# Accumulating DMAs for the sums of a two-gate attention and feed-forward layer, with vector work moved between batches

## The reference

```python
def _bi_wkv(r, k, v, w, u, time_emb):
    tf = sigmoid(sum(time_emb, -1))
    decay = exp(-exp(w)) * (0.5 + 0.5 * tf)
    ek = exp(min(k, 30)); ekv = ek * v
    # a[t] = a[t-1] * decay + ekv[t]; b the same with ek; once forward, once backward in time
    nf, df = scan(step, (ekv, ek)); nb, db = scan(step, (ekv, ek), reverse=True)
    euk = exp(min(u + k, 30))
    num = nf + nb - ekv + euk * v
    den = df + db - ek + euk
    return sigmoid(r) * (num / max(den, 1e-8)) * (0.8 + 0.2 * tf)

# attention: qkv = x @ w_qkv.T + b_qkv; causal softmax(q k / 4) v; @ w_out.T + b_out
# ffn: w -> clip(round(w / mean|w|), -1, 1) * mean|w|; (silu(x @ up) * (x @ gate)) @ down
```

## Time and profile before

| | |
|---|---|
| median of 3 runs | 182.76 us (182.74 to 183.18) |
| the profiled execution, its whole time | 182.91 us |
| its span (first to last instruction) | 181.1 us |
| outside the span | 1.8 us |
| DVE busy | 156.2 us, 86% of the span |
| PE busy | 147.6 us, 82% |
| ACT busy | 114.7 us, 63% |
| POOL busy | 51.1 us, 28% |

### The profile page before, as it was taken

One profiled execution on the slowest core, in us unless ns is written; L12 is line 12 of the kernel. 1 busy time (PEld: TensorE's weight loads), 2 busy tenths in 40 slices (PEclk: granted clock), 3 DMA queues, 4 the chain that ended last, 5 costly groups with the idle time before them and its releaser, 6 DMA issues. The chain is left out here.

```text
span 181.1 us, 3815 instructions
## 1 busy us (share of the span) xinstructions
PE 147.6 (82%) x1544; PEld 97.6 (54%) x1544; DVE 156.2 (86%) x262; ACT 114.7 (63%) x181; POOL 51.1 (28%) x49
## 2 busy tenths in 40 slices
PE   0008597973999889999899689997998999997991
PEld 0008483331348656764576357744764676785880
DVE  0699958999999979999998999999769999986672
ACT  2638756999777743589357634883593348885550
POOL 8700032999700049340000194400002223000000
PEclk9999789999699999999999999999999999999999
DMA  4999204000000400000132000000420000010001
GB/s 100 360 430 424 108 29 145 4 0 2 0 5 0 173 5 0 0 5 0 58 103 76 0 4 0 2 4 4 144 87 0 0 5 4 4 62 2 4 0 58
DMA packets 5706, 10.91 MB, mean 60 GB/s; under 512 B 760, under 2 KB 4024, under 8 KB 5304
## 3 DMA queue, kind: packets, MB, share of 16 engines
q1 hardware_dynamic: 5400, 10.52, 15.4%
q10 hardware_dynamic: 288, 0.14, 0.5%
HBM read 6.43 MB, written 1.05 MB: 41 GB/s over the span
## 5 line engine op out<-in xcount | busy, mean ns | idle before, releaser
L245 POOL TENSOR_TENSOR extra<-extra,k_t 128x512 f32<-128x512 f32 x7 | 8.9, 1268 | 84.3 <-DVE fwd L589 40.9
L676 DVE TENSOR_REDUCE row_max<-wide 128x4 f32<-128x1024 f32 (+1 forms) x24 | 28.8, 1216 | 0.6 <-PE wide L1039 0.6
L437 ACT ACTIVATE silu<-attn_ps,up_scale 128x256 f32<-128x256 f32 x24 | 11.2, 473 | 24.6 <-PE attn_ps L986 22.1
L399 ACT ACTIVATE probs<-wide 128x1024 f32<-128x1024 f32 x24 | 23.9, 1020 | 3.2 <-PE wide L1064 2.6
L589 DVE TENSOR_TENSOR_SCAN fwd<-decay,ek 128x256 f32<-128x256 f32 x32 | 21.1, 704 | 0.0
L601 DVE TENSOR_TENSOR_SCAN bwd<-ek,decay 128x255 f32<-128x255 f32 x32 | 21.1, 706 | 0.0
L270 POOL TENSOR_TENSOR hid_lo<-hid,hid_hi 128x512 f16<-128x512 f32 x9 | 12.4, 1380 | 14.3 <-ACT hid_hi L444 14.3
L1184 PE MATMUL wide<-ones 128*128 128x128 f32 x24 | 4.5, 369 | 14.1 <-DVE fwd L776 14.1
L986 PE MATMUL attn_ps<-x_lo,w_tern 128*128 128x256 f16 x96 | 13.9, 273 | 1.2 <-DVE x_lo L701 1.2
L986 PE MATMUL attn_ps<-x_hi,w_tern 128*128 128x256 f16 x96 | 14.3, 274 | 0.0
L1034 PE MATMUL wide<-mask_qk,identity_b 128*128 128x256 bf16 (+1 forms) x48 | 11.0, 311 | 3.6 <-DMA stack<-halves 1.9
(11 more groups left out here) (144 smaller groups left out, 343.3 us busy)
## 6 DMA issues: line engine op xcount, KB each, us to landing
stack<-halves SPq DMA_DIRECT2D x24, 128.0 KB, 2.1
w_raw<-wup_d SPq DMA_DIRECT2D x1, 1024.0 KB, 11.5
w_raw<-wgate_d SPq DMA_DIRECT2D x1, 1024.0 KB, 13.2
w_raw<-wdown_d SPq DMA_DIRECT2D x1, 1024.0 KB, 15.0
out_d<-x_t SPq DMA_DIRECT2D x4, 256.0 KB, 2.3
wqkv<-wqkv_d SPq DMA_DIRECT2D x1, 768.0 KB, 7.2
k_t<-k_d SPq DMA_DIRECT2D x1, 768.0 KB, 8.6
x_t<-x_d SPq DMA_DIRECT2D x1, 768.0 KB, 10.0
```

What stands on the lines that cost most here:

```text
L399: nc.scalar.activation(probs[:, j, :], flat(wide[j % 2][:, :, :]), ACT.Exp, scale=SOFTMAX_SCALE).then_inc(prob_done, 1)
L437: nc.scalar.activation(silu[:, e % 2], up, ACT.Silu, scale=up_scale[:, 0:1]).then_inc(silu_done, 1)
L676: nc.vector.tensor_reduce(out, src, AX.X, ALU.max).then_inc(max_done, 1)
```

## The change

Seven edits, in neutral terms:

1. Ten of the large adds become DMAs that GpSimd issues with `accum_op=ALU.add`: `send_extra` and `send_backward` for gate 0 of batches 2 and 3 (`by_dma`) and gate 1 of batches 0 to 2. A gate's second DMA waits for the first. `sums` of these gates and their `add_extra` leave the compute engines. Gate 1 of batch 3 keeps both adds on the vector engine.
2. The two products of batch 0 (`values_of_keys(0)`, `extra_products(0, 0)`) move from the vector engine to GpSimd, and half of the small decay and gain instructions stand behind `first_gate(0)`.
3. Scans move between turns: gate 0's of the next batch leave the block of `maxima` and `gate`, and stand at the border; in the last turn gate 1's backward scans stand around the border, and its forward scans inside the block.
4. `ffn_input` now writes f32 `x2`; ScalarE copies it to `x2_hi` (`high_input`); `low_input` subtracts.
5. ScalarE: `minus_maxima(0)` moves ahead of the second `ternary_weights`, the third goes to turn b = 1 ahead of the first silu, `key_exp(3)` moves two exponentials later. Its list has the second gate's reciprocal ahead of the row sums' in every turn, as before.
6. TensorE: three more filler products of `ones` behind the first twelve, released by `recn_done[0]`; in turn b = 1 the first `up_gate` products of `x2_hi` stand ahead of the scores.
7. The last network's last block is split in two pieces (`tail_halves`).

```diff
@@ when a DMA adds, and who waits for it
+        def by_dma(c, b):
+            return b >= 2 if c == 0 else b < B - 1
+        def wait_summed(engine, c, b):
+            if by_dma(c, b):
+                engine.wait_ge(sum_in[c], 16 * (b - 1 if c == 0 else b + 1))
+            else:
+                engine.wait_ge(sum_done[c], b + 1 if c == 0 else 1)
...
@@ gpsimd
-            def add_extra(c, b):
+            def send_extra(c, b):
                 pool.wait_ge(prod_done[c], b + 1)
                 pool.wait_ge(fwd_done[c], 4 * b + 4)
-                nc.gpsimd.tensor_tensor(fwd[c][:, :, :], fwd[c][:, :, :], extra[c][:, :, :],
-                                        ALU.add).then_inc(fwd_extra[c], 1)
+                pool.dma_start(fwd[c][:, :, :], extra[c][:, :, :], accum_op=ALU.add).then_inc(extra_in[c], 16)
+            def send_backward(c, b):
+                wait_extra_added(pool, c, b)
+                pool.wait_ge(bwd_done[c], 4 * b + 4)
+                pool.dma_start(fwd[c][:, :, :], bwd[c][:, :, :], accum_op=ALU.add).then_inc(sum_in[c], 16)
...
+            values_of_keys(0)
+            extra_products(0, 0)
             pool.wait_ge(blank, 3)
...
@@ scalar
+            def high_input(b):
+                for ct in range(CT):
+                    act.wait_ge(x2_done, 2 * b + ct + 1)
+                    nc.scalar.activation(x2_hi[:, ct, :], x2[:, ct * T:(ct + 1) * T],
+                                         ACT.Copy).then_inc(x2hi_done, 1)
...
@@ vector, ffn_input and low_input
-                    nc.vector.scalar_tensor_tensor(x2_hi[:, ct, :], x2[:, part], 1.0, wkv2[:, b, part],
-                                                   ALU.add, ALU.mult).then_inc(x2hi_done, 1)
+                    nc.vector.scalar_tensor_tensor(x2[:, part], x2[:, part], 1.0, wkv2[:, b, part],
+                                                   ALU.add, ALU.mult).then_inc(x2_done, 1)
+            def low_input(b):
                 dve.wait_ge(x2hi_done, 2 * b + 2)
-                nc.vector.scalar_tensor_tensor(x2[:, :], x2[:, :], 1.0, wkv2[:, b, :],
-                                               ALU.add, ALU.mult).then_inc(x2_done, 1)
...
@@ vector, bound_denominator
-                dve.wait_ge(sum_done[c], b + 1)
+                wait_summed(dve, c, b)
...
@@ vector, the last network's last block
+            def tail_halves(e):
+                f, i = B - 1, e % EG
+                dve.wait_ge(hid_done, ET * f + e + 1)
+                dve.wait_ge(down_done, NG * f + 2)
+                nc.vector.tensor_copy(hid_hi[:, 1, i], hid[:, 1, i]).then_inc(last_hi, 1)
+                dve.wait_ge(last_hi, B + i)
+                nc.vector.tensor_tensor(hid_lo[:, 1, i], hid[:, 1, i], hid_hi[:, 1, i],
+                                        ALU.subtract).then_inc(last_lo, 1)
...
@@ tensor
+            pe.wait_ge(recn_done[0], 1)
+            for _ in range(3):
+                nc.tensor.matmul(wide[0][:, 0, 0:P], ones[:, :], ones[:, :], start=True, stop=True)
             pe.wait_ge(wqkv_in, 16)
```

More of the change, by code:

```diff
@@ L824, in _ @@
                     if b > 1:
+                        if more:
+                            backward(0, b + 1, 0, (1,))
                         first_product(1, f)
@@ L876, in _ @@
+                    forward(1, b, 1)
+                    forward(1, b, 0)
+                    refine(0, b + 1)
+                    gate_first(b + 1)
+                    first_wkv(b + 1)
+                    backward(1, b, 1)
+                    backward(1, b, 0)
+                    finish(f)
                     if b + 2 < B:
                         forward(0, b + 2, 1)
-                    if more:
-                        low_halves(b + 1, 0)
+                        forward(0, b + 2, 0)
@@ L905, in _ @@
                     dve.wait_ge(bo_done, 1)
-                    forward(0, 2, 1)
-                    backward(0, 2, 1)
+                    for half in (1, 0):
+                        forward(0, 2, half)
+                    for half in (1, 0):
+                        backward(0, 2, half)
                     first_product(1, 0)
```

155 lines of the change are left out of this document (83 added, 72 removed).

## The result

The changed kernel is slower by 1.3%: 184.45 us median (183.49 to 185.25, 4 runs) against 182.75 us (181.34 to 183.18, 4 runs) of the kernel before on the same chip, a ratio of 1.013 (95% interval 1.007 to 1.018). The forecast was 180.4 us. The profiled execution took 183.49 us, with a span of 181.7 us.

The account below looks back on a forecast made before the run. DVE bounds up to 62 us; later TensorE, ScalarE and chains of waits also bind. Terms -1.0 - 0.1 - 0.1 - 1.15 - 0.2 = -2.55, rounded to -2.5, from the profiled 182.91 give 180.4 us; range 178.9 to 184.8.

Parts of the forecast that it names:

- the price D: Time from GpSimd's issue of one adding 512 KB DMA to its semaphore: taken as 4.3 us, from rates giving 3.0 to 7.
- the order of the two reciprocals: Turn 1, gate's and row sums' reciprocals on ScalarE: same order in both kernels, so given nothing.
- The lateness of the three scans: Border 2 to 3: three scans before the residual make it 1.0 us late, so only 1.25 of 2.2 us comes through.
- the start: Up to 31 us: fillers give the first keys full clock, -1.65; with GpSimd product delays net -1.0 us (-1.6 to +0.9).
- The sign that the forecast itself named for being wrong: A bound waiting for a DMA by several us in turns 1 and 2, or a slow scan beside a GpSimd product.
- turn 3 and the end: Last turn: `ffn_input` -0.25, last reciprocal at most 0.15 to 0.25 better, split last block +0.05; together -0.2 us.
- The plain-transfer estimate of 3.2 us: Skill's figure for a plain 512 KB DMA, 2.0 us plus bytes over 436 GB/s; by it the sum is 0.2 better.
- the DMAs are too slow: Rival: gate 1's two DMAs in sequence, at D = 6, lose 2.15 us in turn 1, 2.8 in turn 2; 185.4 us, chance 0.19.
- 2D against 10.25: Turn 1, gate 1: its two successive DMAs may take 10.25 us together before the bound waits for them.
- 118.15 + 2D against 127.75: Turn 2: gate 1's second DMA lands at 127.75 for D = 4.3, and at 118.15 + 2D beyond D = 5.3.
- the two reciprocals end at the same place: Turn 1: gate's and row sums' reciprocals, 1.2 and 1.25 us, both follow the bound, so they do not help; turn -0.1.
- The block's -1.45: Turn 2 block: scan pair ahead of the first row maximum and TensorE's 1.25 us wait go, saving 1.45 us.

Follow-up runs that it names:

- experiment 12: Kernel before plus the change's three filler products: 181.76 us, ratio 0.999; kernel before, unchanged, profiled again: 181.33 us, span 179.5; filler kernel profiled again: 181.15 us.
- experiment 1: Changed kernel with the 256 KB store of a batch issued one turn later: 183.36 us, ratio 1.011 to the kernel before.
- experiment 8: Changed kernel with the store one turn later and stack DMAs of batches 2 and 3 held until gate 1's second DMA landed: 182.91 us, ratio 1.006.
- experiment 9: Changed kernel with 32 tiny TensorE products at the start, shifting its instruction fetches: times scatter from 182.44 to 188.2 us.
- experiment 3: Changed kernel with the row sums' reciprocal ahead of the gate's on ScalarE and the normalization earlier on DVE: 184.07 us, ratio 1.011 to the kernel before.
- experiment 4: Changed kernel with gate 1's three backward scans of batch 3 moved behind the last halves: 184.12 us, ratio 1.012 to the kernel before.
- experiment 10: Changed kernel with store later, row sums' reciprocal first, three scans moved and last block unsplit, plus 32 tiny start products: 183.05 us, ratio 1.003 to the kernel before.

## Why the prediction was wrong

Most of the miss is in turns 1 and 2, where the sum had a gain of 0.1 and of 1.15 us and the runs show a loss of 2.0 and of 0.4. Two terms failed there: the price D of the second DMA (4.3 us taken; from the end of the scans to the landing it was 7.2 us in turn 1 and 5.4 in turn 2), and the order of the two reciprocals, which was put at nothing. The lateness of the three scans was sized rightly, but set against a gain that didn't come. A third term, the start, was built on one execution. The sign that the forecast itself named for being wrong, a bound that waits for a DMA by several us in turns 1 and 2, came: 2.29 and 3.02 us.

Against the kernel before at the same clock (experiment 12), what each stretch adds, in us; the brackets have the times at which it ends:

| | forecast | measured |
|---|---|---|
| start and turn 0 (residual 59.48 to 59.54) | -1.1 | +0.1 |
| turn 1 (97.43 to 99.49) | -0.1 | +2.0 |
| turn 2 (134.16 to 136.58) | -1.15 | +0.4 |
| turn 3 and the end (span 179.5 to 181.7) | -0.2 | -0.2 |

**The start term failed, though its mechanism was seen.** Against the profile that I had, the residual at the border 0-1 came 1.54 us earlier (61.08 to 59.54), more than my -1.1. But the 1.65 us of slow keys, on which the term was built, were the chance of one execution: without the fillers they were fast too in one run, and the kernel before has them fast in another profile. The three runs shown before the change all lay near the upper group. I took one profile's granted clock for a property of the kernel.

**The price D was right for a DMA alone and wrong for the one that counts.** 4.4 us measured, 4.3 taken. The plain-transfer estimate of 3.2 us from the Trainium skill's "DMA: Bandwidth & Descriptors" (section "Anatomy of one DMA — SWDGE (gpsimd) path") differs from the measurement for an adding one, and the measurement decides. In turn 1 gate 0's bound came 1.9 us ahead of the forecast's 80.2, at 78.33. With everything shifted by that, gate 1's bound was reached 0.2 us later than forecast, at 91.49, and the landing was 3.1 us later: 0.2 for the scans ahead, 0.55 for GpSimd to start behind the last of them (scans end 86.56, issue 87.11), which I had not counted, and 6.6 us in place of 4.3. Of those 2.2 us above 4.4, 1.6 are the two fetches and 0.6 the store (experiments 1, 8, 9). The rival "the DMAs are too slow" had the right place, a second DMA that lands after the bound is reached, and a sum of 185.4; its mark, D at 6 for all of them, was not what happened. By its own formulas, 2D against 10.25 and 118.15 + 2D against 127.75, D = 6 loses 1.75 and 2.4 us and not 2.15 and 2.8, so its sum should have been 184.6. The small terms of turn 1, too, add up to -0.2 and not to the -0.1 that the sum took.

**Turn 1's "the two reciprocals end at the same place"** held only while the bound was on time. In the change it is 2.29 us late, and everything queued behind the gate's reciprocal is late with it. I had said that the order of the two reciprocals is the same in both kernels and given it nothing. It was the same, and no longer harmless: experiment 3 takes 1.1 us off the residual of turn 1 by the order on ScalarE and DVE alone.

**Turn 2.** The block's -1.45 was right: from the residual to the first row maximum 4.36 us before (99.03 to 103.39) and 2.89 after (99.49 to 102.38). The border was not. The forecast's times here leave out the gain at the start. The scans ahead of the last DMA ended at 124.44 where I had 123.45 (0.6 us handed over by turn 1, 0.4 lost inside the turn), then came 0.55 us for GpSimd to start and 4.9 us of landing: 129.87 in place of 127.75, and the normalization at 132.82 in place of 130.8. The three scans' lateness was foreseen at 1.0 us, and experiment 4 measures 1.1; but it was set against 2.2 us of gain at the border, most of which didn't come.

**Turn 3 and the end** came as forecast in their sum. The split of the last block cost 0.2 us in place of 0.05 (from the last residual, at 166.57, to the last `finish` 11.69 us, before 11.46).

**The clock at the borders** was in no step. TensorE's idle of 2.8 us, the price of the late DMA, is paid a second time in the executions in which the clock falls behind it. This would explain why the medians differ by 1.7 us where the two profiled spans differ by 0.6; it is not shown, since no such execution of the changed kernel was profiled.

## What to carry to other kernels

Work moved to a DMA with an adding write leaves the engine, but its result comes 4.4 to 6.8 us after the issue in this case, by what else the DMA engines carry; what is queued in order behind the step that reads it, on any engine, should be ready later than it, or go first. When two delays end at the same step, undo them together before one is called harmless. And before a gain is built on a slow stretch of one profile, see whether the kernel's own times lie in two groups.

## What the runs showed of the hardware

- An adding DMA of 512 KB within the chip lands in 4.4 to 4.5 us from GpSimd's issue when nothing disturbs it, of which GpSimd is busy 0.87 us, and it starts 0.55 us behind the scan it waits for. Beside the 256 KB store and four stack DMAs it took 4.9 us, beside three stack DMAs and no store 4.5.
- Two fetches of instructions in its time made 6.0 us of 4.5 with nothing else of the program in flight, with a tail of single packets, as of one engine that ends last. One fetch of queue 8 made 5.2 to 6.5 us of 4.4 to 4.5 in six DMAs that it was moved into (experiments 9 and 10), and a stack DMA of 128 KB went from 2.1 to 3.7 us.
- Queue 8 makes 12 fetches in this kernel, one for about every 256 of TensorE's 3100 instructions, so that 128 more of them at the start (32 products, each seen as two matmuls and two weight loads) were enough to move its later fetches out of one DMA and into others.
- Behind an idle of 2.1 to 2.8 us ahead of the same projection, TensorE kept the full clock in four profiles (2.76, 2.37, 2.72, 2.30 us) and fell to 1.2 GHz for 3 to 4 us in four others (2.15, 2.75, 2.09, 2.58 us), of kernels that differ little.
